# Twenty-one of 49 destination tiles summed from stored count blocks in place of twenty

## The reference

```python
x_neigh = segment_sum(edge_w[:, None] * x[edge_src], edge_dst)   # layer 0, weighted
agg     = segment_sum(h[src], dst)                               # layer 1, three times, unweighted
m       = segment_sum(h[src], dst) * rsqrt(deg_in)[:, None]      # layer 2, unweighted
e1      = segment_sum(edge_val[:, None] * x[edge_col], edge_row) # layer 3, weighted
```

## Time and profile before

| | us |
|---|---|
| three timed runs, median (lowest to highest) | 5903.73 (5901.43 to 5907.27) |
| the profiled execution, its own time | 5894.2 |
| its span, first to last instruction | 5892.6 |

### The profile page before, as it was taken

How to read it: one execution, slowest core, us unless ns; L and a number is a source line. 1 busy time by engine, 2 the same in 40 slices (tenths; PEclk the granted TensorE clock), 3 DMA queues, 4 the chain that set the end, 5 groups by cost and what they waited for, 6 DMA issues and landing times. The chain is left out here.

```text
span 5892.6 us, 105131 instructions
## 1 busy us (share of the span) xinstructions
PE 5007.4 (85%) x36007; PEld 4163.1 (71%) x36007; DVE 3910.6 (66%) x14561; ACT 1656.7 (28%) x4651; POOL 3895.5 (66%) x3767
## 2 busy tenths in 40 slices
PE   5888887679998899969888889997899966888887
PEld 3766766467776788857777668885788843666665
DVE  5777767468777799947878735447888845444553
ACT  3767776311111111111222200000233312333332
POOL 6766667767777677757666767775334452777776
PEclk8999988799999999979999989998999967999998
DMA  5433344677778788886666777774899952443333
GB/s 156 133 117 126 128 128 132 195 211 225 226 223 256 230 242 244 243 283 202 202 196 199 233 221 216 216 219 140 271 321 325 313 158 80 111 112 112 112 112 97
DMA packets 648787, 1129.31 MB, mean 192 GB/s; under 512 B 128154, under 2 KB 459032, under 8 KB 645532
## 3 DMA queue, kind: packets, MB, share of 16 engines
q0 software_dynamic: 213632, 629.15, 37.5%
q1 hardware_dynamic: 434618, 493.35, 25.5%
HBM read 994.85 MB, written 128.55 MB: 191 GB/s over the span
## 5 line engine op out<-in xcount | busy, mean ns | idle before, releaser
L2274 POOL DMA_INDIRECT ring<-planes,REC x1566 | 1565.5, 1000 | 642.9 <-issue 501.9
L2371 PE MATMUL PS<-HH,pick 128*128 128x256 bf16 (+1 forms) x7836 | 987.0, 275 | 80.8 <-DMA pick<-dense_blocks 45.0
L2371 PEld LDWEIGHTS PS<-HH,pick 128*128 128x128 bf16 x7836 | 766.4, 99 | 206.5 <-DMA pick<-dense_blocks 50.7
L2274 POOL DMA_INDIRECT ring<-in_x,REC x555 | 595.2, 1072 | 267.0 <-issue 148.5
L2350 PE MATMUL PS<-ring,pick 128*128 128x256 f32 x2160 | 631.2, 418 | 156.0 <-DMA ring<-table,REC 102.5
L2274 POOL DMA_INDIRECT ring<-table,REC x525 | 505.5, 963 | 262.5 <-issue 256.7
L2347 PE MATMUL PS<-ring,pick 128*128 128x256 bf16 (+1 forms) x4698 | 626.0, 276 | 53.1 <-DMA ring<-planes,REC 52.1
L2274 POOL DMA_INDIRECT more<-planes,REC x522 | 524.3, 1004 | 180.2 <-issue 150.3
L2350 PEld LDWEIGHTS PS<-ring,pick 128*128 128x128 f32 x2160 | 408.7, 204 | 311.1 <-DMA ring<-table,REC 146.0
L2371 PE MATMUL PS<-HH,ring 128*128 128x256 bf16 (+1 forms) x3924 | 512.0, 276 | 54.8 <-DMA ring<-dense_blocks 34.9
L2347 PEld LDWEIGHTS PS<-ring,pick 128*128 128x128 bf16 x4698 | 453.3, 98 | 143.9 <-DMA ring<-planes,REC 71.6
(11 more groups left out here) (377 smaller groups left out, 9383.6 us busy)
## 6 DMA issues: line engine op xcount, KB each, us to landing
HH<-in_L_gnn_w SPq DMA_DIRECT2D x256, 512.0 KB, 5.7
pick<-dense_blocks SPq DMA_DIRECT2D x480, 160.0 KB
ring<-dense_blocks SPq DMA_DIRECT2D x240, 160.0 KB
HH<-planes SPq DMA_DIRECT2D x64, 576.0 KB, 7.3
dense_blocks<-HH SPq DMA_DIRECT2D x20, 1568.0 KB, 6.0
planes<-pick SPq DMA_DIRECT2D x147, 192.0 KB
ring<-planes,REC POOLq DMA_INDIRECT x1566
table<-HN SPq DMA_DIRECT2D x147, 128.0 KB
```

The source lines that it names most:

```text
L2274: pool.indirect_dma_start(slot_row(k, slot, 0, RP if dense else D), None, planes[k] if dense else tables[k], bass.IndirectOffsetOnAxis(ap= ...
L2371: last = mm(bank(5 + n % 2, w), block, plane(m, t, w), start=t == 0 and m == 0, stop=t == NT - 1 and m == 2, skip_group_check=True)
```

## The change

`DENSE` takes 21 tiles in place of 20, spread evenly: [2, 4, 6, 8, 11, 13, 15, 17, 20, ..., 44, 46]. All else follows from that list or makes room for it. Passes 1 to 4 have 28 sparse tiles: 168 steps in place of 174, of which 156 have dense blocks in place of 162, now 6.60 a step. Pass 0 still has 246 steps and 8 weighted tiles, but 21 builds, one every 10 steps. Of the other tiles 15 are sorted in pass 1 as before, and 13 in pass 3 in place of 14. Pass 5 has ten weighted tiles as before, some with another number. The other edits let the waits hold for an odd number of dense tiles and keep a buffer's turn in pass 5.

```diff
-DENSE = [t for t in range(NT - 2) if t * 20 // (NT - 2) != (t + 1) * 20 // (NT - 2)]
+DENSE = [t for t in range(NT - 2) if t * 21 // (NT - 2) != (t + 1) * 21 // (NT - 2)]
...
-BIN_AT = [2 + 21 * i // 2 for i in range(ND)] + [3 + 11 * (i % 15) for i in range(NT - ND)]
+BIN_AT = [2 + 10 * i for i in range(ND)] + [3 + 11 * (i % 15) for i in range(NT - ND)]
...
-BUILD_AT = [2 + 21 * i // 2 for i in range(ND)] + [PACE * i for i in range(len(WEIGHTED[5]))]
+BUILD_AT = [2 + 10 * i for i in range(ND)] + [PACE * i for i in range(len(WEIGHTED[5]))]
...
-                        sp.wait_ge(s_as[j], 16 * ND // 2)
+                        sp.wait_ge(s_as[j], 16 * len(range(j, ND, 2)))
...
-                    to, lanes = WXS[fw % OWN], BINS5[u % 2]
+                    to, lanes = WXS[fw % OWN], BINS5[(u - ND) % 2]
```

More of the change, by code:

```diff
@@ L3071, in block_build @@
                         else:
-                            last = v.tensor_scalar(WXD[fw % OWN][:, j * 2 * P:(j + 1) * 2 * P], iota1, BINS5[u % 2][:, 0, c], BINS5[u % 2][:, 3, c],
+                            last = v.tensor_scalar(WXD[fw % OWN][:, j * 2 * P:(j + 1) * 2 * P], iota1, BINS5[(u - ND) % 2][:, 0, c], BINS5[(u - ND) % 2][:, 3, c],
                                                    ALU.is_equal, ALU.mult)
@@ L3361, in one_pass @@
                         for j in range(2):
-                            dve.wait_ge(s_as[j], 16 * ND // 2)
+                            dve.wait_ge(s_as[j], 16 * len(range(j, ND, 2)))
                         dve.wait_ge(s_wq, NB * len(WEIGHTED[0]))
```

## The result

| | us, median (lowest to highest) |
|---|---|
| before, 5 runs | 5905.71 (5901.43 to 5907.27) |
| after, 5 runs | 5883.5 (5871.58 to 5896.42) |
| ratio, 95% interval | 0.9961 (0.9943 to 0.9979) |

The change makes the kernel 0.4% faster. I had forecast 5919 us, 0.25% slower. The profiled execution took 5883.5 us (before 5894.2), its span is 5881.8 us.

The account below looks back on a forecast made before the run. TensorE was taken to bound passes 2, 3 and 4, GpSimd pass 1, and VectorE the builds of pass 0. +21 - 18 + 3 + 0 + 9 = +15 us on 5903.7 gave 5919 us, range 5892 to 5939.

Parts of the forecast that it names:

- the first failed step: Pass 0: the added plain build costs VectorE 21.5 us that nothing hides; +21 us, ends +3 and +30.
- the sixteen builds of mixed kind: Pass 0: pressed into 160 steps from 168, bound by work, so eight steps' time moves behind them; nothing won or lost.
- from step 160 to 204: Pass 0: four builds in place of three in a VectorE-bound stretch, so the added build counts in full; +21 us.
- the build is hidden in pass 0: Rival: gathers cover the added build, +3 us in place of +21; total 5901 us; chance 0.14.
- the second failed step: Pass 3: TensorE's added +10.2 us, less 8.4 for one sort and a little at the end; 0, ends +10 and -23.
- pass 3 goes by VectorE: Rival: added matmuls fall into TensorE's 61.1 us of waits, pass 3 loses what VectorE loses, -23 us; 5890 us; chance 0.12.
- Pass 4: TensorE sets the pace: +10.2 us of matmuls less 1 us of idle time; +9 us, ends +2 and +11.
- Pass 1: GpSimd sets the pace: 18 gathers fewer give at most 22.6 us; -18 us, ends -22.6 and -5.
- Pass 2: TensorE sets the pace: +10.2 us, about 7 us won behind the dense blocks; +3 us, ends +10 and -8.
- The rule against it: Pass 4: by the weight loads' share TensorE has 12% free; the prediction held 27 matmuls without a gap against it.

Follow-up runs that it names:

- spacing alone: The kernel before with its 20 builds of pass 0 ten steps apart in place of ten and a half: 5890.67 us, ratio 0.9989 on a quick chip.
- 14 and 14: The changed kernel with 14 sorts in pass 1 and 14 in pass 3 in place of 15 and 13: 5882.23 us, 0.9976 on a quick chip.
- The pair with 13 sorts: The changed kernel with tile 24 built in pass 0 but summed by gathers (5884.28 us), and the changed kernel itself (5883.5 us).
- built and not used: The changed kernel with tile 24 built and sorted in pass 0 but summed by gathers in passes 1 to 4: 5884.28 us, 0.9985 on a quick chip.

## Why the prediction was wrong

**Pass 0, the first failed step (+21 forecast, -0.8 measured).** Two sentences of it fail. The first: the sixteen builds of mixed kind "are bound by work and not by steps, so eight steps' worth of time moves behind them and is neither won nor lost". The windows of pass 0 (steps 0 to 60, 60 to 120, 120 to 162, 162 to 204, 204 to the first product of pass 1) of the kernel before:

```profile
25.80:314.10 288.30, 220.51 (x1016) 170.18 (x1017) 192.37 (x637) 168.46 (x453) 205.82 (x190) 0.89 0.50 146
314.10:613.80 299.70, 251.36 (x1232) 205.25 (x1231) 210.86 (x710) 217.88 (x591) 194.85 (x180) 0.92 0.40 126
613.80:822.10 208.30, 176.15 (x863) 144.39 (x862) 147.05 (x492) 150.97 (x410) 140.01 (x127) 0.92 0.39 125
822.10:1014.50 192.40, 150.37 (x736) 120.53 (x735) 145.97 (x487) 131.49 (x360) 134.27 (x125) 0.89 0.42 134
1014.50:1207.10 192.60, 117.24 (x439) 77.38 (x438) 80.14 (x292) 61.34 (x166) 128.69 (x129) 0.77 0.58 184
sum 1181.30, PE 915.62 PEld 717.73 DVE 776.39 ACT 730.14 POOL 803.64; mean PE 183.12 PEld 143.55 DVE 155.28 ACT 146.03 POOL 160.73
```

of the kernel with the spacing alone, the second and the last two stretches and the sum:

```profile
317.50:611.90 294.40, 251.94 (x1268) 207.59 (x1267) 216.60 (x723) 225.08 (x610) 202.66 (x182) 0.93 0.41 129
...
817.70:1008.80 191.10, 145.55 (x706) 115.30 (x705) 147.48 (x497) 134.28 (x368) 141.14 (x124) 0.87 0.43 134
1008.80:1197.50 188.70, 118.94 (x395) 74.25 (x394) 63.56 (x246) 43.65 (x118) 125.13 (x132) 0.76 0.59 190
sum 1171.50, PE 913.96 PEld 712.71 DVE 776.39 ACT 731.39 POOL 816.65; mean PE 182.79 PEld 142.54 DVE 155.28 ACT 146.28 POOL 163.33
```

and of the kernel after:

```profile
26.20:316.80 290.60, 223.53 (x1022) 171.85 (x1023) 198.75 (x646) 173.00 (x465) 208.23 (x187) 0.87 0.49 143
316.80:614.00 297.20, 253.54 (x1269) 208.74 (x1268) 216.91 (x723) 225.20 (x610) 199.96 (x182) 0.92 0.40 128
614.00:820.20 206.20, 177.40 (x895) 146.31 (x894) 149.62 (x505) 155.29 (x420) 136.15 (x127) 0.93 0.41 127
820.20:1013.30 193.10, 146.94 (x707) 116.16 (x706) 150.78 (x512) 135.38 (x371) 142.88 (x126) 0.86 0.44 137
1013.30:1206.30 193.00, 119.83 (x441) 77.46 (x440) 81.67 (x298) 63.43 (x171) 129.95 (x130) 0.77 0.60 190
sum 1180.10, PE 921.24 PEld 720.53 DVE 797.73 ACT 752.30 POOL 817.17; mean PE 184.25 PEld 144.11 DVE 159.55 ACT 150.46 POOL 163.44
```

The first two kernels do the same work, VectorE 776.39 us in both, and the one with the closer spacing is 9.8 us shorter. In its second stretch VectorE does 5.7 us more in 5.3 us less. So that stretch was not full of VectorE's work; it held waits between engines.

Before against after says it without the kernel in between. Of the 21.3 us that VectorE works more, 15.0 lie in front of step 162 (550.3 to 565.3), where the time fell by 2.3 us (796.3 to 794.0); 4.8 and 1.5 lie in the two stretches behind it, which grew by 0.7 and 0.4. VectorE's work is not what these stretches go by. What they go by, the chain of work that ended last tells (`--critical`). The chain of the kernel before breaks off in pass 5, so here is that of the kernel with the spacing alone, steps 0 to 162:

```profile
by line: PE PS L2433 12.5%; issue 10.5%; PE PS L2350 10.2%; PE PS L2393 8.9%; ACT HH L2779 5.8%; POOL ring L2274 5.6%; ACT HH L2741 4.4%; ACT HH L2793 4.3%; DMA HH<-in_x 3.9%; PE PS L2489 3.1%; ACT HH L2748 2.3%; ACT HH L2781 2.1%; ACT HH L
```

Summed over all its lines, TensorE has 301 us of these 792, ScalarE 210 and VectorE 101; behind step 162 GpSimd has 107 of 380 and VectorE 39. So where weighted builds run, the path is TensorE's (L2433, the sums of the weighted tiles, stands first) and ScalarE's (one-hots and copies of the builds, L2779, L2741 and L2793).

Two of the waits between engines, in the second stretch, of the kernel before:

```profile
DVE ring L3134 <- ACT ring L2816: 22.7, 10, 3.1
...
PE PS L2393 <- ACT HH L2781: 18.5, 10, 2.6
```

and with the spacing alone:

```profile
PE PS L2393 <- ACT HH L2781: 10.2, 5, 5.0
DVE ring L3134 <- ACT ring L2816: 8.6, 5, 2.3
```

Others grew: VectorE's wait for ScalarE's L2810 went from 12.0 to 16.5 us. That these waits follow from where a build falls against the end of a tile is my reading; no run isolates it. What the runs show is that the gain doesn't grow with closeness: with 21 builds, pass 0 is shorter at ten and a quarter steps than at ten. Which position is best I can't say.

The second: "from step 160 to 204 there are four builds now in place of three, and that stretch is VectorE-bound with either". The build's work I had right: VectorE's sum grows by 21.3 us (776.39 to 797.73), my 21.5. But against the kernel with the spacing alone 18.1 us of them lie behind step 204 (63.56 to 81.67), in steps that go by gathers and where VectorE is busy 34 to 42% of the time. That stretch grows by 4.3 us and the one ahead of it by 2.0. Counted from that kernel, the last build lengthens a row of overlapping builds and doesn't make it denser. The count of builds was off as well: five begin from step 160 on where four did, though the difference is one either way. The build therefore comes near the rival "the build is hidden in pass 0", for which I had worked out +3: it measured 8, or 6 behind step 162, where I had +21; and the spacing, which I had put at nothing, gave 6 (medians on one chip) to 10 us (profiles). I had given that rival 0.14 because VectorE's 21 us were "nowhere free", and the row that says otherwise was on the table: 33.80 of 81 us without a build.

**Pass 3, the second failed step (0 forecast, -20.7 measured).** "TensorE again: +10.2". The chain of work that ended last in pass 3, again of the kernel with the spacing alone, which in this pass is the kernel before:

```profile
by line: PE PS L2371 14.2%; issue 6.9%; PE PS L2347 6.4%; PE PS L2474 4.5%; DVE ST L3194 4.4%; DVE HH L3011 3.9%; DVE HH L2991 3.6%; DMA pick<-dense_blocks 3.2%; DVE HH L2994 3.2%; POOL ring L2274 2.9%; DVE pick L2950 2.8%; PE PS L2489 2.7%
```

Summed over all its lines, VectorE has 377 us of these 769, TensorE 235, ScalarE 45 and GpSimd 28. So TensorE is on the path for less than a third of the pass. The sort taken away was priced well, 8.4 us against 8.4 and 5.7 measured. What the tile alone does to the dense stretch, 14 sorts in both, spacing alone and then 14 and 14:

```profile
2614.00:3341.90 727.90, 629.35 (x5286) 542.94 (x5284) 554.77 (x2000) 146.62 (x452) 495.33 (x483) 0.93 0.69 203
```

```profile
2608.80:3326.10 717.30, 623.94 (x5379) 544.50 (x5378) 550.54 (x1980) 145.67 (x448) 477.70 (x467) 0.95 0.69 204
```

with the waits of TensorE for ScalarE's copy in the first:

```profile
PE PS L2474 <- ACT TZT L2690: 63.7, 31, 6.1
```

and in the second:

```profile
PE PS L2474 <- ACT TZT L2690: 65.2, 22, 5.5
```

There are 93 more matmuls, and their busy time is 5.4 us less, at a mean granted clock of 0.95 in place of 0.93. I took each matmul at the median distance to the next of its line and shape at full clock. So measured, to about 1 us, the work grows from 583.2 to 593.4 us, the 10.2 of the forecast (by its making, since it is the same count at the same price). What is lost at half clock (1.2 GHz) falls from 32.8 to 19.5, and what TensorE is idle from 111.9 to 104.4. The pair with 13 sorts gives the same: work +10.2, half clock -10.6, idle -8.2. The step charged each added matmul to the pass as if TensorE were its bound, in a pass where it is idle for 112 us of 728 and loses 33 to its clock.

The rival "pass 3 goes by VectorE" doesn't hold as it stands either. Its waits of TensorE for ScalarE were not filled; they are fewer and longer, and their sum stays at 60 to 65 us. And the pass doesn't lose what VectorE loses: the sort taken away took 16.0 us of work from VectorE in the dense stretch (554.8 to 538.8, spacing alone against built and not used) and 8.4 from the pass, while the tile from blocks took 4.2 from VectorE (rows above) and 13.3 from the pass. That its -23 is near the -20.7 is chance: its "19.7 us" for a sort is worked out nowhere, the 21.5 of pass 0 being a sort with its one-hots. In the chain GpSimd falls from 28 us to nothing with the tile from blocks (14 sorts), and VectorE from 377 to 369, while TensorE rises from 235 to 254: the path changes hands between all of them. What ties the pass's length to its number of steps no run isolates. That the clock stays up longer because TensorE pauses less is argued from these rows, not shown.

**What held.** Pass 4: TensorE's work there grows by 10.1 us and the pass by 8, none of it hidden, as GpSimd was as fast and not slower. In 580 us of its dense stretch GpSimd now waits 38 times for a product where it waited 18 times, and TensorE waits 0.4 us for blocks. Pass 1: -14 for -18, within the ends that I gave; its waits for gathers went from 27.2 to 3.1 us, those for blocks grew by 6.2, and TensorE is busy for 608 of 644 us, 94%, where I had 97%. Pass 2: +2.1 in the profile and +3 in the means, with +3 forecast, but by luck. The last dense matmul ends at 2551.5 us before and at 2543.5 after, so that the dense stretch took 609.2 and then 614.7 us, +5.5 where I had +10.2 (TensorE's idle time in it fell from 8.7 to 4.5 us), and what follows took 45.3 and then 41.9, -3.4 where I had -7. Both terms were about twice too large, and the errors cancel.

**The rule against it.** By the rule of the Trainium skill that I had weighed (Perfetto Trace Analysis, "Identifying the Most-Contended Engine"), read by its weight loads alone, TensorE would have had 12% of pass 4 free. The section names MFU (the matmul work done, as a share of the peak) beside the weight loads; the prediction left that out, and it is not worked out here. Had there been that room, the pass would have got up to 22.6 us shorter by the gathers that it lost. It got longer by 8, so the measurement decides against the weight loads' share as a measure of room here: in pass 4, where matmuls start 0.110 us apart and TensorE is busy for 613.5 of 616.4 us, 93 more of them took 9 us of busy time and 8 us of the pass, though weight loads had been busy for only 88% of it.

## What to carry to other kernels

Count a busy engine's work as path only where it is never idle, and ask the chain of the last work, not the busy share, who is on the path. Here the same exchange of 54 matmuls and 18 gathers for 147 matmuls cost 8 us in a pass where TensorE was busy for 99.5% of the time, and gave 11 to 13 in one where it was idle for 15%. An added background job of 21 us on VectorE cost 8 us, in a pass whose path VectorE holds for an eighth to a tenth. And when a change has to move a job's position to make room, price that by itself: it gave 6 to 10 us here, as much as the job cost, and on late chips it cost up to 12.

A version of the changed kernel with its builds ten and a quarter steps apart has the lowest median on the quick chip 3 and on the late chip 13 (0.9955 and 0.9898 of before). On chip 3 it takes 0.9973 of the kernel with 14 and 14 sorts, which has the changed kernel's pass 0. Beside the changed kernel itself it ran on chip 13 alone: 0.9987, within the noise.

## What the runs showed of the hardware

The same program takes 5897 to 5906 us in two groups of runs and 6504 to 6563 us in four, on four other chips, 10 to 11% more, and the change is worth 0.4% on one kind and 0.9 to 1.0% on the other. VectorE, ScalarE and GpSimd are busy as long on either (3911 and 3900, 1657 and 1652, 3895 and 3886 us), TensorE 4% longer (5007 and 5198) at a lower mean granted clock (0.929 and 0.904). What differs most is when the others see that TensorE is done. Kernel before on a quick chip (start us, us, engine and line), the transpose of a tile and the copy of ScalarE that waits for it:

```profile
2206.25 0.42 PE L2465 MATMUL PS<-ident,TZ 128*128 128x128 f32 x2
2206.70 0.38 ACT L2690 ACTIVATE TZT<-PS 128x256 f32<-128x256 f32 x1 [1.38 <-PE PS L2465]
```

and on a late one:

```profile
2422.19 0.42 PE L2465 MATMUL PS<-ident,TZ 128*128 128x128 f32 x2
2425.17 0.38 ACT L2690 ACTIVATE TZT<-PS 128x256 f32<-128x256 f32 x1 [2.58 <-remote]
```

The copy starts 0.03 us after the matmul's end on the first and 2.56 us after it on the second, with ScalarE idle in both. Over the whole kernel, where ScalarE had been idle, this distance is under 0.045 us in 180 of 184 cases on the quick chip and in 44 of 208 on the late one, where its median is 2.1 us. From VectorE to ScalarE (L3196 to L2719) the median is 0.034 us on either. The ends of matmuls in a trace are modelled, so either the signal or the matmuls themselves are late; that stays open. GpSimd on the late chip, pass 2:

```profile
2416.16 0.94 POOL L2274 DMA_INDIRECT ring<-planes,REC  x1 [1.11 <-remote]
2417.41 0.95 POOL L2274 DMA_INDIRECT ring<-planes,REC  x1 [0.30 <-issue]
2418.66 0.95 POOL L2274 DMA_INDIRECT ring<-planes,REC  x1 [0.30 <-issue]
2420.70 0.94 POOL L2274 DMA_INDIRECT ring<-planes,REC  x1 [1.09 <-remote]
```

Groups of three gathers now have a pause of 1.1 us ahead of them (in 730 us of the pass, some 160 groups, 124 pauses of 1.1 us on average, and 26 waits for a product of TensorE). On the late chips a step takes 4.57 to 4.61 us in pass 2 of all nine profiles with 174 steps there, and 4.54 to 4.61 in all five with 168, with more matmuls in each; on the quick chip it goes from 3.76 to 3.91. So on a late chip six steps fewer are worth 27 us, and passes 1, 2 and 4 gave 21, 28 and 22 (pass 3 only 7). The same exchange that cost pass 4 8 us on the quick kind gives it 22 here, where a step's length doesn't grow with its matmuls: a gain forecast from one chip's profile need not hold on another.
